# A mixture-of-experts gather on Trainium2: one fp32 product, or three bf16 products whose parts sum to the same rows

## The reference, cut to what matters

```
topk_w, topk_ids = _grouped_topk(x @ gate_w, bias)      # 6 of 64 experts per token
order = jnp.argsort(topk_ids.reshape(-1)); ...           # pos: the place in the expert's queue
buf = zeros((E, CAP + 1, H)).at[se, slot].set(x[tok])[:, :CAP]          # the gather
h   = silu(einsum('ech,ehf->ecf', buf, w_gate)) * einsum('ech,ehf->ecf', buf, w_up)
out = einsum('ecf,efh->ech', h, w_down)                  # H = 256, F = 96
y   = segment_sum(out[se, min(pos, CAP-1)] * valid * w, tok)             # back to the tokens
return y + (silu(x @ ws_gate) * (x @ ws_up)) @ ws_down
```

## Time and profile before

| | |
|---|---|
| runs, us | 1241.92, 1246.28, 1247.13; median 1246.28 |
| the profiled execution, us | 1239.18 |
| its span, first to last instruction | 1237.2 |
| mean granted TensorE clock | 0.946 |
| PE busy | 1073.2 us, 87% of the span |
| DVE busy | 692.8 us, 56% |
| ACT busy | 479.4 us, 39% |
| DMA moved | 84.38 MB, mean 68 GB/s |
| gather L3329, PE | 128 records, 26.4 us busy |

### The profile page before, as it was taken

How to read it: one execution, slowest core, us unless ns; L and a number is a source line. 1 busy time by engine, 2 the same in 40 slices (tenths; PEclk the granted TensorE clock), 3 DMA queues, 4 the chain that set the end, 5 groups by cost and what they waited for, 6 DMA issues and landing times.

```text
span 1237.2 us, 22875 instructions
## 1 busy us (share of the span) xinstructions
PE 1073.2 (87%) x9353; PEld 753.3 (61%) x9353; DVE 692.8 (56%) x1534; ACT 479.4 (39%) x1056; POOL 192.9 (16%) x186
## 2 busy tenths in 40 slices
PE   6988899986975999999999997989999471777998
PEld 5866566655754555655555665676666251676886
DVE  4544357772333767665666642637567867555332
ACT  1111147771320344555555674534444230121222
POOL 0003100000001100000000000006886886000000
PEclk9999999997997999999999999999999685978999
DMA  9012300004001200000000002014454443005551
GB/s 382 13 70 84 120 2 2 2 2 165 1 1 58 106 1 1 2 2 2 2 2 2 2 2 84 1 59 111 126 151 125 121 131 89 15 1 212 214 211 54
DMA packets 16183, 84.38 MB, mean 68 GB/s; under 512 B 3153, under 2 KB 3665, under 8 KB 12369
## 3 DMA queue, kind: packets, MB, share of 16 engines
q1 hardware_dynamic: 7888, 57.75, 12.2%
q0 software_dynamic: 8192, 25.17, 7.2%
HBM read 82.65 MB, written 0.26 MB: 67 GB/s over the span
## 4 chain that ended last, share of the span: by engine, by line
PE 67%; DVE 13%; POOL 11%; issue 5%; ACT 3%; DMA 1%; POOLq 0%; SPq 0%; DVEq 0%; ACTq 0%
POOL L2F_rows L2512 8%; PE L2X_bank_ring L1771 7%; PE L2X_bank_ring L1787 6%; PE L2X_bank_read L1801 6%; PE L2X_bank_ring L1710 4%; PE L1X_banks_scores L916 3%; PE L2X_bank_ring L1719 3%; PE L0X_bank_k L457 2%; PE L3F_bank_y L3380 2%; PE L0X_bank_moments L468 2%; PE L3F_bank_gathered L3329 2%; DVE x L2743 2%; PE L3F_bank_gate_up L3340 2%; PE L1X_bank_proj L893 2%; PE L1A_bank_qk L1181 2%
## 5 line engine op out<-in xcount | busy, mean ns | idle before, releaser
L2068 DVE TENSOR_REDUCE L2X_max_parts<-L2X_bank_ring 128x1 f32<-128x512 f32 x256 | 158.3, 683 | 85.7 <-PE L2X_bank_ring L1771 85.7
L1979 ACT ACTIVATE L2X_context_exp<-L2X_bank_ring 128x384 f32<-128x384 f32 (+1 forms) x384 | 144.1, 462 | 62.4 <-PE L2X_bank_ring L1787 59.6
L2512 POOL DMA_INDIRECT L2F_rows<-in_L2F_embed_dram,L2F_expert x128 | 131.6, 1028 | 59.7 <-issue 36.3
L1771 PE MATMUL L2X_bank_ring<-L2X_context_kT,L2X_q_masked 32*128 32x512 f32 x512 | 96.9, 630 | 0.0
L1024 ACT ACTIVATE L1X_probs<-L1X_clipped,L1X_drop,L1X_keep 128x1024 f32<-128x1024 f32 x64 | 77.6, 1237 | 30.7 <-DVE L1X_clipped L1084 23.5
L1084 DVE TENSOR_SCALAR L1X_clipped<-L1X_banks_scores 128x1024 f32<-128x1024 f32 x64 | 75.4, 1219 | 24.6 <-PE L1X_banks_scores L916 22.9
L1787 PE MATMUL L2X_bank_ring<-L2X_q_and_max,L2X_context_kT 32*128 32x384 f32 (+1 forms) x768 | 85.9, 497 | 0.0
L1801 PEld LDWEIGHTS L2X_bank_read<-L2X_context_exp,L2X_context_v_ones 128*32 128x32 f32 x2048 | 50.2, 109 | 43.8 <-issue 33.4
L1801 PE MATMUL L2X_bank_read<-L2X_context_exp,L2X_context_v_ones 128*32 128x128 f32 x2048 | 75.8, 277 | 1.1 <-ACT L2X_context_exp L1979 0.8
L2743 DVE SCALAR_TENSOR_TENSOR x<-L2F_rows,L2F_expert_weight,x 128x256 f32<-128x256 f32 x128 | 62.4, 487 | 4.6
L221 POOL TENSOR_TENSOR L2A_ln_var_inv_sqrt<-L2A_ln_var_plus_eps,consts 128x2 f32<-128x2 f32 x1 | 0.7, 697 | 356.5 <-DVE L2A_ln_var_plus_eps L216 356.5
(11 more groups left out here) (625 smaller groups left out, 2068.8 us busy)
## 6 DMA issues: line engine op xcount, KB each, us to landing
L3F_expert_weights<-in_L3F_experts_dram SPq DMA_DIRECT2D x16, 1280.0 KB, 5.7
L1A_groups<-in_L1A_groups_dram SPq DMA_DIRECT2D x3, 1536.0 KB, 9.6
ctxT<-in_ctxT_dram SPq DMA_DIRECT2D x8, 512.0 KB, 11.1
L0X_tokens<-in_L0X_tokens_dram SPq DMA_DIRECT2D x8, 512.0 KB, 15.3
slot<-in_L1A_dram SPq DMA_DIRECT2D x1, 3584.0 KB, 11.3
slot<-in_L0F_dram SPq DMA_DIRECT2D x1, 3072.0 KB, 11.4
slot<-in_L2A_dram SPq DMA_DIRECT2D x1, 3072.0 KB, 10.9
slot<-in_L2F_dram SPq DMA_DIRECT2D x1, 2476.5 KB, 8.8
```

The costliest lines, as they stand in the source:

```text
L1771: nc.tensor.matmul(bank[:, :], qm[32 * g:32 * g + 32, b, c, j, :], cT[32 * g:32 * g + 32, s % 3, blk * 512:(blk + 1) * 512], start=True, s ...
L1979: nc.scalar.activation(ex[:, n % NE, g, 0:width(s)], bank_of(s_e, done(n) + g + 1)[:, 0:width(s)], ACT.Exp, scale=SCALE).then_inc(s_e, 1)
L2068: nc.vector.tensor_reduce(parts[:, j, g, blk:blk + 1], bank_of(s_ft, n)[:, :], AX, ALU.max).then_inc(s_ft, 1)
L2512: pool.indirect_dma_start(out=rows[:, r, k, :], out_offset=None, in_=env.dram["L2F_embed"], in_offset=bass.IndirectOffsetOnAxis(idx[:, b, ...
```

## The change

Two things change in L3F, and nothing outside it.

`here` becomes bf16, which holds 0 and 1 exactly. And `xn` is split by four new DVE instructions into three bf16 parts: the first is `xn` rounded to bf16, the second is the remainder rounded to bf16, the third is what remains of that; three times 8 bits of significand hold the 24 of an fp32 number. `gather(j)` becomes 12 bf16 matmuls (2 channel halves, 3 parts, 2 token halves) in place of 4 fp32 ones, summed in the same PSUM columns. A new semaphore, `s_parts`, lets PE's first `gather` wait for the parts; DVE waits for `xn` ahead of the split. `shares` now reads `here` as bf16 beside the fp32 weights.

```
     NB = 3
-    here = L.sb("in_seat", [P, NB, B, PER * CAP])
+    here = L.sb("in_seat", [P, NB, B, PER * CAP], BF16)
+    NPART = 3
+    part, rest = L.sb("xn_parts", [P, NPART, B, D], BF16), L.sb("xn_rest", [P, B, D])
...
             for k in range(KC):
-                for b in range(B):
-                    i = nc.tensor.matmul(bank_ga[:, k * PER * CAP:(k + 1) * PER * CAP], head.xn[:, b, k * P:(k + 1) * P],
-                                         here[:, j % NB, b, :], start=(b == 0), stop=(b == B - 1))
+                for m in range(NPART):
+                    for b in range(B):
+                        i = nc.tensor.matmul(bank_ga[:, k * PER * CAP:(k + 1) * PER * CAP], part[:, m, b, k * P:(k + 1) * P],
+                                             here[:, j % NB, b, :], start=(m == 0 and b == 0), stop=(m == NPART - 1 and b == B - 1))
             i.then_inc(s_ga, 1)
...
         turn_hidden(0)
+        pe.wait_ge(s_parts, 1)
         gather(0)
...
         head.vector(dve, chain)
+        dve.wait_ge(head.s_norm, B)
+        chain(nc.vector.tensor_copy(part[:, 0, :, :], head.xn[:, :, :]))
+        chain(nc.vector.tensor_tensor(rest[:, :, :], head.xn[:, :, :], part[:, 0, :, :], ALU.subtract))
+        chain(nc.vector.tensor_copy(part[:, 1, :, :], rest[:, :, :]))
+        nc.vector.tensor_tensor(part[:, 2, :, :], rest[:, :, :], part[:, 1, :, :], ALU.subtract).then_inc(s_parts, 1)
 
         dve.wait_ge(s_re, 1)
```

More of the change, by code:

```diff
@@ L3295, in layer_L3F @@
              "gathered", "gathered_copied", "gate_up_done", "tanh_ready", "silu_ready", "hidden_ready", "hidden_turned",
-             "hiddenT_ready", "share_turned", "shareT_ready", "down_done", "rows_copied", "shared_added", "job_added")
+             "hiddenT_ready", "share_turned", "shareT_ready", "down_done", "rows_copied", "shared_added", "job_added", "xn_split")
     (s_chain, s_r, s_re, s_sel, s_rank, s_clear, s_here, s_share, s_ga, s_xg, s_gu, s_e, s_a, s_h, s_t, s_hT, s_st, s_sT, s_o, s_eo,
-     s_ys, s_y) = (L.sem(n) for n in names)
+     s_ys, s_y, s_parts) = (L.sem(n) for n in names)
     env.prefetch(L, None)
```

## The result

| | before | after |
|---|---|---|
| runs, median us | 1243.67 (22 runs) | 1241.79 (22 runs) |
| ratio | | 0.9975, interval 0.9963 to 0.9986 |
| second comparison, median us | 1246.95 (35 runs) | 1242.30 (12 runs) |
| its ratio | | 0.9969, interval 0.9942 to 0.9996 |
| profiled execution / span, us | 1239.18 / 1237.2 | 1237.62 / 1235.4 |

What follows compares the result with a forecast made beforehand. PE's streams were taken to bound 14 of the loop's 16 turns, at full clock. Savings of 4.1 + 0 + 0.4 = 4.5 us, taken from the median of 1246.3, gave 1241.8 us, range 1236.5 to 1249.

Steps and rivals of the forecast that it cites:

- One pass per bf16 column: PE's gather: a bf16 record streams its columns once where fp32 takes two passes; 0.99 us against 1.30 per job.
- the step of 0.083: Gather in the loop: 192-column bf16 records follow each other every 0.083 us at 2.4 GHz, loads hidden behind streams.
- the 72%: Chance given to the main forecast of 1241.8 us, with its own range of 1238 to 1246.
- First load of the gather: Start of each gather on PE: the unhidden first load takes 0.05 us instead of 0.10.
- `copy_rows` decides: Turns 1 to 14: `add_job` waits for DVE's copy, so each turn gives 0.29 us, not PE's 0.36; 4.1 us altogether.
- Turn 0: Loop's first turn, without `add_job`: `turn_hidden(1)` waits for the hidden product, so a faster gather gives 0 to 0.03 us.
- Job 0's gather 0.4: Gather ahead of the loop at half clock: 0.4 us less, between 0 and 0.7.
- The split costs nothing: Four DVE instructions after the norm: 2.33 us, at most 2.85, inside 3.29 us of DVE idle time.
- Rival 1: Gather loads set the pace, 0.107 to 0.113 us per step; time 1246.3, give or take 0.5; chance 18%.
- rival 2: Gather loads not hidden but in series, a step of 0.136 us or more; 1251 to 1262.6 us; chance 7%.
- rival 3: DVE's split overruns its cover, or bf16 needs two passes in the gather, then 1256 us; chance 3%.
- The sum: Whole kernel 4.5 us less: 4.1 from turns 1 to 14, 0 from turn 0, 0.4 from job 0's gather.

Runs made afterwards that it cites:

- e2: Changed kernel with `copy_rows` moved between silu's two products on DVE; turn 5.821 us, layer 116.6 us, ratio 0.9957 to the kernel before.
- e3: Kernel before plus the DVE split and PE's wait for it, gather still fp32; turn 6.193 us, layer 122.5 us, ratio 0.9997.
- e0: Changed kernel profiled and timed again without edits; turn 5.908 us, layer 118.0 us, ratio 0.9969 to the kernel before.
- e5: Changed kernel, each gather product cut into two of 96 columns, operand loaded each time; turn 5.910 us, ratio 0.9961 to the kernel before.
- e9: Changed kernel, each gather product cut into four of 48 columns, operand loaded each time; turn 6.095 us, layer 120.7 us, one run.
- e8: Changed kernel with GpSimd's three memsets put off until the split is done; turn 5.909 us, layer 118.1 us, ratio 0.9953 to the kernel before.

## Why the prediction was right, step by step

- One pass per bf16 column, and the step of 0.083: measured 0.083. The loads are hidden, as taken; by a wide margin that I did not know of, since they cost at most 0.025. The grounds were thinner than the 72% sounds. L1F's stream, from which I took it, has 0.21 us for each load to hide in; that a load fits into 0.083 rested on halving the length of a record, 106 ns. At full clock these records last 95 to 99 ns and not 53, and they are no price at either clock. So this step came out right for a reason that I did not have.
- First load of the gather 0.05: its first product lasts 0.256 against 0.246, so 0.01, where fp32 had 0.10 (0.430 against 0.326). The stream of the gather is thus 0.40 shorter, from 1.40 to 1.00 us between its first product and `add_job`'s; with the copy moved `add_job` itself takes 0.03 more than before (1.755 against 1.727 from its first product to the next stage's). PE alone would have gained 0.37 instead of 0.36, which e2 shows (6.193 - 5.821).
- `copy_rows` decides, a turn gives 0.29, and 0.07 us of gap opens: 0.284 and 0.08. Turns 1 to 14 gave 4.0 us.
- Turn 0: I said 0 to 0.03; from the loop's first tanh to its second it went from 3.63 to 3.52 us, 0.11. I had read the wait from the load of `turn_hidden(1)` at 1136.42. Its products stood behind the gather all the same, which held PE to 1136.72: they end 1.67 us after the first tanh before the change, and 1.58 after it.
- Job 0's gather 0.4: 0.45 between e3 and e0. In the two profiles by themselves that stretch went from 5.62 to 5.76 us, as the half clock lay otherwise.
- The split costs nothing: right by e3. The two sizes in it were off: the split took 2.57 and not 2.33 us, and the cover was 2.85 to 3.05 and not 3.3 us in all profiles with the split but that of e5 (3.49), since the router's products ran at full clock for longer in them (1.10 to 1.30 us for the eight records of L334, against 1.55 before and 1.74 in e5). With my own upper bound of 2.85 for the four instructions it would just have run over. That `seats` and `shares` keep their time was right: 0.55 us each, before and after.
- Rival 1 (loads at 0.107) and rival 2 (loads in series) are refuted by the step of 0.083 itself, and further by e5 and e9; rival 3 by e3 and by the records. The rule of the Trainium skill, page "TensorE: Matmul & The Clock Gate", section "LDWEIGHTS (loading the stationary operand)", does not hold here as a spacing at either clock, and the estimate of 0.107 for this stream falls by either of the sections cited there. The 106 ns in the earlier trace rows, which I had read as agreeing with it, was the length of a record and no price: pairs of a bf16 load and a narrow product follow each other every 0.040 us at half clock and every 0.025 at the full one (e9).
- The sum: 4.5 us less was forecast, as 4.1 + 0 + 0.4. Between e3 and e0, whose half clock lies alike, it was 4.0 + 0.11 + 0.45, of 4.55 us in all. The 4.3 and 4.5 against the profile before contain 0.34 and 0.24 us ahead of job 0's gather, which the change did not make.
- The whole time: the ratios are 0.9975 and 0.9969, and 4.5 us would be 0.9964, inside both intervals. The middle of both lies 0.6 to 1.4 us short of it. The split is not it (e3). Two other kernels whose turns and layer are those of the change, e5 and e8, came out at 0.9961 and 0.9953, or 4.8 and 5.8 us: the four values lie on both sides of 4.5, so nothing shows that anything is missing.
- That 1241.8 us were forecast and 1241.79 measured is luck. The forecast stood on a median of three runs, 1246.28; the median of 22 runs before is 1243.67, and the medians differ by 1.9 us and not by 4.5.

## What to carry to other kernels

Before pricing a faster stage, follow the consumer's other inputs: here the copy of the experts' rows allowed the next stage to end 0.28 us sooner, and that margin, not the 0.36 us of saved streaming, was the gain of a turn. After such a change look at whatever stood just behind the old bound; moving one copy by one place on DVE, worth next to nothing before, then gave 1.4 us more. And where PE pauses ahead of short dependent products, look at the granted clock that they get: filling the pause gave 2.5 us.

## What the hardware showed that I had not expected

- A bf16 load of a 128 x 128 operand and its product follow each other every 0.025 us when the product is 48 columns, at full clock, and every 0.043 with 96; an fp32 load allows 0.113.
- A conversion from fp32 to bf16 of 128 x 512 on DVE took 0.66 us beside a GpSimd memset and 0.43 without; the memset of 256 columns 0.47 and 0.31.
